# Six rotary attention layers: halves swapped on VectorE instead of by DMA, sine products on GpSimd, two norm buffers, a new order of the small phases, and TensorE's loop unrolled

## The reference

```
x = attn_layer(shift_tokens(x)) + x      # shift: the upper 64 features come from the token before
x = ffn_layer(shift_tokens(x)) + x
attn_layer: qkv = x @ Wqkv               # 128 -> 3 * 1024: 16 heads of 64 features
            q, k = l2norm(q) * qs, l2norm(k) * ks
            q = q * cos * scale + rotate_half(q) * sin * scale      # k with 1 / scale
            softmax over the own and the previous window of 32 tokens, times v, @ Wo
ffn_layer:  layernorm, a, gate = xn @ W1 + b1 (341 each), (a * gelu(gate)) @ W2 + b2
rotate_half(x) = concat(-x2, x1) of the two halves of a head's 64 features
```

## Time and profile before

| | us |
|---|---|
| median of 3 runs (2575.57 to 2611.07) | 2578.05 |
| the profiled execution | 2560.68 |
| its span | 2558.9 |
| TensorE busy, share of the span | 1969.0, 77% |
| VectorE busy | 1180.6, 46% |
| ScalarE busy | 1023.7, 40% |
| GpSimd busy | 963.2, 38% |
| granted TensorE clock, mean share of full speed | 0.89 |
| DMA: packets' share of 16 engines | 42.6% |

### The profile page before, as it was taken

One profiled execution on the slowest core, in us unless ns is written; L12 is line 12 of the kernel. 1 busy time (PEld: TensorE's weight loads), 2 busy tenths in 40 slices (PEclk: granted clock), 3 DMA queues, 4 the chain that ended last, 5 costly groups with the idle time before them and its releaser, 6 DMA issues.

```text
span 2558.9 us, 96456 instructions
## 1 busy us (share of the span) xinstructions
PE 1969.0 (77%) x44564; PEld 1154.0 (45%) x44592; DVE 1180.6 (46%) x1198; ACT 1023.7 (40%) x1377; POOL 963.2 (38%) x621
## 2 busy tenths in 40 slices
PE   2999865778878877877788788778777877787775
PEld 1444433444444444444444444444444444444442
DVE  3344533455444445435444444454454454545442
ACT  1344533343443444434344434344343444334431
POOL 4222313434443333634345433346343354424330
PEclk9777968889889989989899899899898998989996
DMA  4000004555545555545545455555455455445441
GB/s 112 1 2 2 2 30 131 140 133 143 132 131 137 141 134 134 153 109 154 138 122 152 131 138 141 138 133 151 110 151 136 122 135 139 136 118 133 124 112 40
DMA packets 134835, 295.44 MB, mean 115 GB/s; under 512 B 23061, under 2 KB 48019, under 8 KB 127251
## 3 DMA queue, kind: packets, MB, share of 16 engines
q1 hardware_dynamic: 134418, 289.00, 42.6%
HBM read 177.54 MB, written 4.46 MB: 71 GB/s over the span
## 4 chain that ended last, share of the span: by engine, by line
PE 45%; DMA 15%; DVE 15%; issue 10%; ACT 8%; POOL 4%; SPq 3%; ACTq 0%; DVEq 0%; POOLq 0%
DMA r_all<-r_rows 7%; PE bank L996 4%; PE ring L694 4%; PE bank L901 3%; DMA t_sin<-sin_raw 3%; PE bank L877 3%; PE ring L952 3%; DVE rot L1500 3%; DMA w_raw<-in_L_ffn_Wqkv 3%; PE bank L1027 3%; PE ring L696 3%; PE ring L979 3%; PE ring L695 3%; DVE sin_raw L1496 2%; PE bank L798 2%
## 5 line engine op out<-in xcount | busy, mean ns | idle before, releaser
L598 POOL TENSOR_TENSOR rot<-rot,t_sin 128x1024 f32<-128x1024 f32 x192 | 461.4, 2403 | 1162.9 <-DMA t_sin<-sin_raw 1162.9
L1496 DVE TENSOR_TENSOR sin_raw<-ring,tab_sb 128x1024 f32<-128x1024 f32 x192 | 234.7, 1222 | 521.0 <-ACT sq L1218 441.1
L1218 ACT ACTIVATE sq<-ring 128x1024 f32<-128x1024 f32 x192 | 196.8, 1025 | 498.3 <-PE ring L696 498.3
L1507 DVE SCALAR_TENSOR_TENSOR rot<-r_all,rot 128x2048 f32<-128x2048 f32 x96 | 219.7, 2289 | 329.3 <-DMA r_all<-r_rows 329.2
L901 PE MATMUL bank<-wv_sb,x_tok 128*32 128x128 f32 x6144 | 235.8, 294 | 25.7 <-issue 25.7
L694 PE MATMUL ring<-xs_parts,w_hi 128*128 128x512 f32 x384 | 184.1, 479 | 86.8 <-issue 42.6
L605 POOL TENSOR_TENSOR o_feat<-o_feat,inv_all 128x1024 f32<-128x1024 f32 x96 | 234.9, 2468 | 33.3 <-DMA inv_all<-inv_rows 33.3
L1500 DVE TENSOR_TENSOR rot<-ring,tab_sb 128x1024 f32<-128x1024 f32 x192 | 233.0, 1213 | 0.0
L901 PEld LDWEIGHTS bank<-wv_sb,x_tok 128*32 128x32 f32 x6144 | 172.2, 117 | 104.4 <-issue 97.5
L1233 ACT ACTIVATE v_sb<-bank 128x512 f32<-128x512 f32 x192 | 114.7, 597 | 219.7 <-PE bank L901 219.5
L979 PE MATMUL ring<-probs,v_sb 32*64 32x64 f32 (+1 forms) x12288 | 168.8, 238 | 33.5 <-issue 33.3
(11 more groups left out here) (147 smaller groups left out, 2924.8 us busy)
## 6 DMA issues: line engine op xcount, KB each, us to landing
t_sin<-sin_raw SPq DMA_DIRECT2D x384, 256.0 KB
r_all<-r_rows SPq DMA_DIRECT2D x192, 512.0 KB, 6.8
inv_all<-inv_rows SPq DMA_DIRECT2D x96, 512.0 KB, 6.2
tab_sb<-in_rotary SPq DMA_DIRECT2D x6, 1024.0 KB, 9.7
w_raw<-in_L_ffn_Wqkv SPq DMA_DIRECT2D x48, 128.0 KB, 5.9
wv_sb<-in_L_ffn_Wqkv SPq DMA_DIRECT2D x12, 256.0 KB, 7.8
wo_sb<-in_L_ffn_Wo SPq DMA_DIRECT2D x6, 512.0 KB, 8.9
x_tok<-state SPq DMA_DIRECT2D x24, 128.0 KB, 6.5
```

The lines of the kernel that those rows point to most:

```text
L598: pool.tensor_tensor(dst, dst, t_sin[:], ALU.add).then_inc(s_rot, 1)
L1496: dve.tensor_tensor(sin_raw[:].rearrange("p a t -> p (a t)"), both, tab_sb[:, at + 2 * TOK:at + 4 * TOK], ALU.mult).then_inc(s_sin, 1)
L1507: dve.scalar_tensor_tensor(out=dst, in0=r_all[:], scalar=NORM_CAP, in1=dst, op0=ALU.min, op1=ALU.mult).then_inc(s_fin, 1)
```

## The change

- `rope` no longer multiplies by the sine. It shuffles the projected pair out of PSUM into `swapped[m % 2]`, neighbouring partitions exchanged (VectorE's stream_shuffle in groups of 32), then makes the cosine product as before. It waits for s_p and for the add two pairs back, not for the square or a swap.
- `squares` reads `swapped` instead of PSUM. `add` on GpSimd multiplies `swapped` in place by the sine table (rolled no longer; its scales follow in four columns), then adds it to `rot`.
- The swap DMAs, `sin_raw` and `t_sin` are gone. `r_norm` and `x_mid` lie in `x_flat`. `r_all` has a buffer for each c.
- TensorE, ScalarE and VectorE bodies have a new order of the feed-forward's steps, of `project`, `norm2`, `turn_max` and `rnorm`. GpSimd makes the next input's split at a body's start and the scaling after the first add.
- SP spreads the inverses in the half in which it stores them, and loads the shifted input a body earlier.
- TensorE's `Fori` is replaced by a Python loop: its bodies are all unrolled.

```diff
+SWAP = [i + 1 - 2 * (i % 2) for i in range(SLOT)]
...
 sq = sb("sq", [P, 2, 2, TOK])
-sin_raw = sb("sin_raw", [P, 2, TOK])
-raw = [sin_raw[:], x_flat[:, 2 * TOK:4 * TOK].rearrange("p (a t) -> p a t", a=2)]
-t_sin = sb("t_sin", [P, 2, TOK])
+swapped = [sb(f"swapped{i}", [P, 2, TOK]) for i in range(2)]
...
-r_all = sb("r_all", [P, 4, TOK])
-r_norm = sb("r_norm", [P, TOK])
+r_all = sb("r_all", [P, 2, 4, TOK])
+r_norm = x_flat[:, 2 * TOK:3 * TOK]
...
-    def swap_halves(m):
-        sp.wait_ge(s_sin, m + 1)
-        if some(m):
-            sp.wait_ge(s_rot, m)
-        for a in range(2):
-            sp.dma_start(t_sin[a:P - 1 + a:2, :, :], sin_raw[1 - a:P - a:2, :, :]).then_inc(s_swap, 16)
+        sp.dma_start(x_shift[0:HALF, s % 2, :], state[0:HALF, at:at + TOK]).then_inc(s_xr[g % 2], 16)
+        sp.dma_start(x_shift[HALF:P, s % 2, 1:TOK], state[HALF:P, at:at + TOK - 1]).then_inc(s_xr[g % 2], 16)
     def store_norms(c, k):
         sp.wait_ge(s_r, c + 1)
         if some(c - 1):
-            sp.wait_ge(s_rb, 32 * (c - 1))
+            sp.wait_ge(s_rb[k], 32 * (c // 2))
         sp.dma_start(r_rows[k, :, :], r_norm[0:P:SLOT // 2, :]).then_inc(s_rd, 16)
     def spread_norms(c, k):
-        if some(c):
-            sp.wait_ge(s_fin, c)
+        if some(c - 1):
+            sp.wait_ge(s_fin, c - 1)
...
     def add(m, par, i):
+        l = m // (PAIRS * SEQS)
+        sin = tab_sb[:, (l % 2) * 4 * TOK + 2 * TOK:(l % 2) * 4 * TOK + 4 * TOK].rearrange("p (i t) -> p i t", i=2)
+        part, dst = swapped[m % 2][:], rot[:, par, i, :, :]
+        if m % (PAIRS * SEQS) == 0:
+            pool.wait_ge(s_tab, l + 1)
+        pool.wait_ge(s_sq, m + 1)
+        pool.tensor_tensor(part, part, sin, ALU.mult).then_inc(s_sin, 1)
+        pool.wait_ge(s_sin, m + 1)
         pool.wait_ge(s_cos, m + 1)
-        pool.wait_ge(s_swap, 32 * (m + 1))
-        dst = rot[:, par, i, :, :]
-        pool.tensor_tensor(dst, dst, t_sin[:], ALU.add).then_inc(s_rot, 1)
+        pool.tensor_tensor(dst, dst, part, ALU.add).then_inc(s_rot, 1)
...
+            if a == 0 and not (last and s == SEQS - 1):
+                shifted_parts(g + 1, (s + 1) % SEQS)
             for i in range(4):
                 if nxt:
                     add(4 * n + 4 + i, 1 - a, i)
                 if s == SEQS - 1 and not last:
                     pool.wait_ge(s_p, PAIRS * g + 4 * a + i + 1)
                     split_pair(l + 1, 4 * a + i)
-                if i == 1 and not (first and s == 0 and a == 0):
+                if i == 0 and not (first and s == 0 and a == 0):
                     scale_out(n - 1, g, 1 - a)
-                if a == 0 and not (last and s == SEQS - 1):
-                    if i == 3:
-                        shifted_parts(g + 1, (s + 1) % SEQS)
...
     def norm2(n, c):
         pe.wait_ge(s_sq, 4 * n + 2 * c + 2)
-        if c == 0:
-            pe.wait_ge(s_ve, 4 * n + 2)
+        if n == 0:
+            pe.wait_ge(s_ve, 2 * c + 2)
+        elif c == 0:
+            pe.wait_ge(s_nm, n)
         else:
-            pe.wait_ge(s_ve, 4 * n + 4)
+            pe.wait_ge(s_ve, 4 * n + 3)
         for t in range(4):
             mm = pe.matmul(N_BANK[SLOT * t:SLOT * (t + 1), :], in_head, sq[:, t // 2, t % 2, :],
...
             pe.wait_ge(s_ve, 4 * n + 1)
         elif t == 2:
-            if some(n):
-                pe.wait_ge(s_nm, n)
-            else:
-                pe.wait_ge(s_ln, 1)
+            pe.wait_ge(s_ln, 2 * n + 1)
+        elif n == 0:
+            pe.wait_ge(s_ve, 3)
         else:
-            pe.wait_ge(s_ve, 4 * n + 3)
+            pe.wait_ge(s_ln, 2 * n + 2)
...
         if not last:
-            pe.wait_ge(s_ln, 2 * n + 3)
+            pe.wait_ge(s_ve, 4 * n + 6)
         else:
             pe.wait_ge(s_lns, n)
...
         if not last:
-            pe.wait_ge(s_ln, 2 * n + 4)
+            pe.wait_ge(s_ve, 4 * n + 8)
         else:
             pe.wait_ge(s_nm, n + 1)
...
     body(1, 1, old=False)
-    with pe.Fori(0, BODIES // 2 - 2) as i:
-        body(2 * i + 2, 0)
-        body(2 * i + 3, 1)
+    for g in range(2, BODIES - 2):
+        body(g, g % 2)
...
     def squares(n, i):
         m = 4 * n + i
-        act.wait_ge(s_p, m + 1)
+        act.wait_ge(s_sw, m + 1)
         if some(2 * n + i // 2):
             act.wait_ge(s_n2, 2 * n + i // 2)
-        act.activation(sq[:, i % 2, :, :], ring[0][:], ACT.Square).then_inc(s_sq, 1)
+        act.activation(sq[:, i % 2, :, :], swapped[m % 2][:], ACT.Square).then_inc(s_sq, 1)
...
-        if some(m):
-            dve.wait_ge(s_swap, 32 * m)
+        dve.wait_ge(s_p, m + 1)
+        if some(m - 1):
+            dve.wait_ge(s_rot, m - 1)
         at = (l % 2) * 4 * TOK
         both = ring[0][:].rearrange("p a t -> p (a t)")
-        dve.tensor_tensor(sin_raw[:].rearrange("p a t -> p (a t)"), both,
-                          tab_sb[:, at + 2 * TOK:at + 4 * TOK], ALU.mult).then_inc(s_sin, 1)
+        dve.stream_shuffle(swapped[m % 2][:].rearrange("p a t -> p (a t)"), both, SWAP).then_inc(s_sw, 1)
         if i == 0 and some(n - 1):
             dve.wait_ge(s_st, 2 * n - 2)
         dve.tensor_tensor(rot[:, a, i, :, :].rearrange("p a t -> p (a t)"), both,
                           tab_sb[:, at:at + 2 * TOK], ALU.mult).then_inc(s_cos, 1)
     def final(n, a, c):
-        dve.wait_ge(s_rb, 32 * (2 * n + c + 1))
+        dve.wait_ge(s_rb[c], 32 * (n + 1))
         dve.wait_ge(s_rot, 4 * n + 2 * c + 2)
         dst = rot[:, a, 2 * c:2 * c + 2, :, :].rearrange("p g i t -> p (g i) t")
-        dve.scalar_tensor_tensor(out=dst, in0=r_all[:], scalar=NORM_CAP, in1=dst, op0=ALU.min, op1=ALU.mult
+        dve.scalar_tensor_tensor(out=dst, in0=r_all[:, c, :, :], scalar=NORM_CAP, in1=dst, op0=ALU.min, op1=ALU.mult
                                  ).then_inc(s_fin, 1)
```

The bodies of SP, TensorE, ScalarE and VectorE, in this order, without their removed lines (eight columns of indent are cut in both):

```diff
+            if l_next is not None:
+                sp.wait_ge(s_v, 8 * SEQS * l + 28 + 4 * a)
+                load_values(l_next, a)
+                for i in range(2):
                     sp.wait_ge(s_w, PAIRS * l_next + 4 * a + i - 1)
                     load_pair(l_next, 4 * a + i)
+            if nxt:
+                store_norms(2 * n + 2, 0)
+                spread_norms(2 * n + 2, 0)
+            if a == 1 and g + 2 < BODIES:
+                shifted_input(g + 2, (s + 2) % SEQS)
+            if s == 0 and not first and a == 1:
+                sp.wait_ge(f_wo, SEQS * l)
+                load_wo(l)
+            if s == 1 and not first and a == 0:
+                sp.wait_ge(s_rot, 8 * SEQS * l)
+                load_w1(l, 1 - par)
+            if s == 1 and not first and a == 1:
+                sp.wait_ge(f_w2, SEQS * l)
+                load_w2(l)
+            if s == 1 and not last and a == 1:
+                sp.wait_ge(s_w1s, l + 1)
+                load_tables(l + 1, 1 - par)
+            if l_next is not None:
+                for i in range(2, 4):
+                    sp.wait_ge(s_w, PAIRS * l_next + 4 * a + i - 1)
+                    load_pair(l_next, 4 * a + i)
             if nxt:
                 store_norms(2 * n + 3, 1)
                 spread_norms(2 * n + 3, 1)
             store_inverses(n, a)
+            spread_inverses(n, a)
...
             n = 2 * g + a
             end = last and a == 1
             gn, an, parn = (g, 1, par) if a == 0 else (g + 1, 0, 1 - par)
+            def step(first, second):
+                (late.get(first, nothing) if a == 0 else mine.get(second, nothing))()
             if not end:
                 project(gn, an, parn, 0)
                 value_tile(gn, an, parn, 0)
+            step("v0", "mean")
             max_scores(n, a, 0)
             if not end:
                 project(gn, an, parn, 1)
             max_scores(n, a, 1)
             if not end:
                 value_tile(gn, an, parn, 1)
+            step("", "var")
+            if not end:
+                project(gn, an, parn, 2)
+            turn_max(n, end)
+            step("v1", "")
+            turned_scores(n, a, 0)
+            step("v2", "")
             if not end:
                 norm2(n + 1, 0)
+                project(gn, an, parn, 3)
                 value_tile(gn, an, parn, 2)
             turned_scores(n, a, 1)
             if not end:
+                norm2(n + 1, 1)
+            step("down", "g0")
+            if not end:
+                value_tile(gn, an, parn, 3)
             if a == 0:
                 mine.get("wo0", nothing)()
             else:
+                mine.get("g1", nothing)()
             sum_probs(n, end)
             attend_local(n, a, 0)
             if a == 0:
                 mine.get("wo1", nothing)()
             else:
+                mine.get("g2", nothing)()
             attend_local(n, a, 1)
     pe.wait_ge(a_state, SEQS)
...
             if not (first and a == 0):
                 attended_out(n - 1, g, 1 - a, 0)
+                attended_out(n - 1, g, 1 - a, 1)
             if not end:
                 squares(n + 1, 0)
                 value_out(n + 1, 1 - a, 0)
```

(22 more changed lines are left out.)

140 lines of the change are left out of this document (27 added, 113 removed).

## The result

The changed kernel takes 2436.46 us (median of 4 runs, 2418.24 to 2462.08) against 2589.77 for the kernel before in the same session (4 runs, 2575.57 to 2611.07): ratio 0.940, 95% interval 0.935 to 0.946. The prediction said 2360 us, 2210 to 2470, faster: sign and range hold. Every ratio here leaves out the executions that a lower clock disturbed, as it did the slowest of the changed kernel's four and the profiled one of e8 (2774.51 us). The profiled execution took 2431.11 us, span 2429.3, mean granted clock 0.904, where the prediction's own sum was 2353.

The account below looks back on a forecast made before the run. TensorE was taken as the bound, interrupted by the other engines. Seams -63, shorter bodies -190 and the layers' extra GpSimd work +45 gave -208, so 2353 us profiled; predicted 2360 us, range 2210 to 2470.

Parts of the forecast that it names:

- slots of TensorE: TensorE's matmul steps, walked start to start: 35.1 us in a first half, 27.1 in a second, 62.2 a body.
- allowance for the clock: TensorE's granted clock falling in waits: 0.2 us added to a first half, 1.1 to a second.
- Seams: Back edges of TensorE's Fori: unrolling removes nine seams of 7.0 us each, -63 us, bounds nothing and -74.
- Issue in straight line: TensorE's instruction-fetch waits outside the seams: 1.8 us a half, from 85 us over 47 halves.
- Rival D: The change only moves its waits: seams become straight-line fetch waits, norms' way ends as before; 2540 to 2580, chance 0.05.
- Second norm: TensorE idles 1.5 us a first half, 3.6 a second, as shuffle 3 waits for GpSimd's add 1; splits and tables +45.
- `final` at the next maxima: TensorE reaches the next maxima at 32, `final` ends at 34.0: 2 us of wait a second half.
- Rope: On VectorE a shuffle out of PSUM replaces the sine product: 1.2 us taken, bounds 1.21 and 2.29, VectorE's work unchanged.
- rival B: Lock and shuffle cost more: shuffle at 2.29 us, +145, or `final` meeting GpSimd operations, +95; 2455 to 2505, chance 0.15.
- C: Slower: shuffle stands behind the add two pairs back and excludes GpSimd, or its product is slow; some 3100 us, chance 0.05.
- the forecast's own band: The predicted time's own interval among the rivals: 2280 to 2430 us, chance 0.56.
- A: GpSimd's order doesn't bind, add 1 always early enough, `final` under the norms' slack: 2175, by the median 2190; chance 0.19.

Follow-up runs that it names:

- e8: The kernel before with the new order of steps, two norm buffers and moved loads and spreads, but old rope and loop: 2741.94 us, ratio 1.055 to the kernel before.
- e1: The changed kernel with TensorE's Fori loop put back, nothing else: 2556.72 us, ratio 0.986 to the kernel before.
- e2: The kernel before with only TensorE's loop unrolled: 2618.56 us, ratio 1.008 to the kernel before.
- e10: The changed kernel with the norms' rows stored and spread as bf16, half the bytes: 2331.93 us, ratio 0.907 to the kernel before.
- e5: The changed kernel with GpSimd's output scaling after the second add, W1 split and table scaling after the fourth: 2480.51 us, ratio 0.953 to the kernel before.
- e6: The changed kernel with GpSimd's output scaling after the second add and table scaling after the fourth, W1 split unmoved: 2432.71 us, ratio 0.937 to the kernel before.
- e12: The changed kernel with one more GpSimd addition of 128x512 per head pair, 1.2 us: 2461.94 us, ratio 0.960 to the kernel before.
- e13: The changed kernel with the norms' first logarithm and exponential ahead of the first exponentials on ScalarE: 2411.91 us, ratio 0.933 to the kernel before.

## Why the prediction held, and where it was 78 us short

The size first. The sum's terms for the steady stretch, worked out from its own parts, against the table above:

| term, 47 halves | predicted | measured |
|---|---|---|
| slots of TensorE, 62.2 x 23.5 | 1462 | 1466 (busy x clock) |
| allowance for the clock, (0.2 + 1.1) x 23.5 | 31 | 111 (1577 - 1466) |
| all waits, (0.5 + 0.2 + 0.7 + 1.5 + 1.8 + 0.2 + 0.7 + 3.6 + 2.0 + 1.8) x 23.5 + 45 | 351 | 346 |
| sum | 1843 | 1923 |

In the sum the miss of 80 us is one term: **the clock**. The prediction took 1.3 us a body; the changed kernel pays 4.7. The kernel before pays 5.5 (1603 - 1474 = 129), and nothing in its profile said that the change would give 100 of these back: the mean clock of the stretch was 0.92 and became 0.93. The slots, estimated at full clock, came out within what the clock's rounding allows (0.005 is 8 us): busy time read off a trace is work over clock, and a walk in full-speed slots must be divided by the clock that it will get.

That the waits' sum was right is luck: by kind they miss by -90 to +71 us, and cancel.

- **Seams, -63.** No 51 us half is left, as said. But the term is no constant: 121 us in the new kernel (e1), a loss in the old (e2). Its price by waits was misread: 48 us, not 67.7, lie in the halves over a seam. The bounds "nothing, and -74" missed the upper end, because the waits of the loop were priced from the old order. Why the loop makes straight-line fetches late too (line 973, 127.9 against 78.1) was not settled.
- **Issue in straight line.** Forecast 1.8 us a half, 85 us, which left out the ten waits of line 696 that do not stand at a seam (19 us); measured 156. Rival D's mechanism (the seams' fetch waits come back in straight-line code) happened in this part, though not its time. The Trainium skill ("Runtime: NRT & Kernel Launch", Instruction fetch mechanics) has the sequencer fetch blocks of 256 instructions by its own DMA queue, a crossing "mostly hidden". The trace agrees as to who is fetching (351 packets, 5.75 MB, 16.4 KB each, on the instruction queue, 1.0% of the engines), but not that it is hidden: with e10's halved spreads the waits at `attend_local` fall from 78.1 to 29.0 us.
- **Second norm, 1.5 and 3.6 a half, with the layers' splits +45**: 165 us forecast, 75 measured in the stretch. Right place, and a cause that e5, e6 and e12 bear out by moving it with GpSimd's order and load (shuffle 3 behind add 1), but too big in its base: line 872 waits 0.2 us a first half where the walk had 1.5, and in a second half without extra work on GpSimd (a layer's first body) 1.3 us where it had 3.6. In the bodies with the split of W1 and with the tables it waits 4.3 and 4.4, with the weights' splits 2.7; over the base that is 7.5 us a layer, 37 in all, near the 45 added. Which slot of the walk made the base too long was not settled; GpSimd's product and add (2409 and 2480 ns) kept their price.
- **Missed: the value tile behind the logarithm**, 60 us. The diff has it: `value_tile` 2 now waits for `s_ln`, and on ScalarE square 2 (which waits for norm 0), exps 0 and only then the logarithm follow, 1.0 + 1.0 + 0.7 us, while TensorE has one `project` of 1.5 to do. The walk took "value 2" for free. e13 moves one line and takes 43 us of it out.
- **`final` at the next maxima, 2 a second half (47)**: measured 15; the norms' way did leave the path more often than the walk had it. The turn, 0.7 a half (33): 17.9. Project behind the cosine, 21: 15.5.
- **Rope.** The shuffle takes 1320 ns, not 1.2 us; 192 x 0.12 = 23 us of VectorE's time, not all of it on the path. Of rival B's prices the lock showed: `final` 2417 ns against 2289, and one add of 4.42 us at most where 2.37 is its median. Shuffle and cosine out of PSUM kept 1320 (1280 to 1355) and 1206 ns beside a GpSimd that is busy 68% of the stretch, so the reading that PSUM operands are free of the lock held, and with it the case against C.

The rivals: the total of 2436 lies 6 us above the forecast's own band and in B's, but B's causes do not make the difference (0.1 us a shuffle; `final` 0.13 us each, 96 times, 12 us in all). A is closer than its time says: GpSimd's order binds mainly in halves with extra work, and taking half of that wait out (e6) gained nothing that can be measured; what keeps the kernel from A's time is the clock, the issue waits and the value tile's wait. C's place shows mildly: the shuffle waits 107.8 us for adds, 30 times, also named as a sign of B, while its lock on PSUM readers does not show at all.
